# A stack of eight layers on one core: attention loops written out, side work of a selective scan moved

## The chip, the cores and the metric

The kernel runs on one core of a Trainium2 chip, as one launch. The metric is the device time of a run in microseconds (us), the median of three. The core has a matrix engine (TensorE, PE in the profile), a vector engine (VectorE, DVE), an activation engine (ScalarE, ACT), GpSimd (POOL) and SyncE (SP), which here issues the DMAs. Each engine works through its own list of instructions in order; they meet through semaphores. Matrix products go to PSUM, eight banks of 128 x 512 fp32.

## What is computed

2048 tokens of width 128 pass through eight layers, each with a layer norm ahead of it and a residual added: softmax attention, a mixture of experts, a selective scan, experts again, linear attention, other experts, gated linear attention, and those experts again. Cut to the two layers that the change touches:

```python
# softmax attention, 16 heads of width 8
keys, queries, values = x @ triu(Wk).T, x @ tril(Wq).T, x @ Wv.T
dot = einsum('bqhs,bkhs->bhqk', queries, keys) * scale
att = softmax(dot, axis=-1)
out = einsum('bhqk,bkhs->bqhs', att, values).reshape(b, t, e)
x = x + out @ Wu.T + bu

# selective scan, d_inner 256, d_state 16
xz = xn @ in_proj_w.T;  x_ssm, z = split(xz, 2)
x_ssm = silu(causal_conv4(x_ssm) + conv_b)
dt, B, C = split(x_ssm @ x_proj_w.T, [8, 24])
delta = softplus(dt @ dt_proj_w.T + dt_proj_b)
def step(h, (x_t, d_t, B_t, C_t)):
    h = exp(d_t * A) * h + (d_t * x_t) * B_t
    y_t = sum over states of h * C_t
y = y + x_ssm * Dp
out = (y * silu(z)) @ out_proj_w.T
```

## The kernel before

All activations stay on the core: 16 tiles of 128 tokens, in 4 chunks of 512. Every stage is one function with a block of code for each engine. The order of an engine's work is the order in which that block is written; there is no scheduler.

**softmax_attention.** It works in slots, one for each of the 16 key or query tiles of each of the 16 heads, 256 in all. The scores of a head are computed twice. In the first pass (`find`, L633) a tile of queries meets all keys, and VectorE takes the row maximum from PSUM in two halves (`maxima`, L828). At a head's end VectorE joins and transposes the maxima (L831, L835), GpSimd cuts them into three bf16 parts (`cut_max`, L534 to L547), and SyncE stores them and loads them into the stack of queries as extra rows (`store_max`, L456, L459). In the second pass (`score`, L648) a tile of keys meets all queries, the maximum already subtracted, into a ring of three banks; ScalarE takes the exponential (`unit`, L751) into a ring of four tiles, and TensorE multiplies it by the values (L665), whose second half of columns is ones, so that the sum for the softmax comes along. A slot of TensorE holds 4 `find`, 4 `score` and the value products, of three different tiles: the scores are `LAG_S` = 19 slots behind the maxima, the values 2 more. At the end of a head ScalarE copies the result out (`evacuate`, L758). Stacks and values have three buffers, so a loop body is three heads, 48 slots. The first body is written out with constants, bodies 1 to 4 are a hardware loop (`Fori`) on TensorE, ScalarE, GpSimd and SyncE, and the last head and the tail of the lag are written out again. VectorE loops head by head, from head 1.

ScalarE's unit, whose two waits come up later, is this (`unit`, L747 to L752):

```python
if not first:
    act.wait_ge(pv_done, j * BODY + (us - (RING - 1)))
for c in range(NC_):
    n = us * NC_ + c
    act.wait_ge(s_done, j * (4 * BODY) + (n + 1))
    nc.scalar.activation(probs[...], core.ps[:, S_BANK + n % S_RING, :], ACT.Exp)
```

**selective_scan.** Four chunks of 512 tokens, each 16 rounds (one for each state s), each round in two halves d of 128 channels. In a round ScalarE writes exp(delta * A) to PSUM (L1522), GpSimd multiplies delta * x by the row of B (L1279, B's rows come from DRAM through SyncE), VectorE runs the scan along the tokens (L1633) and multiplies the result by C (L1644), which TensorE has spread over the partitions (`spread_c`, L1355). TensorE adds the products of all states up in PSUM (`add_up`, L1362). ScalarE can be one round ahead of VectorE, GpSimd two.

Beside the rounds, at rounds set by numbers in the code, goes the side work. For z of this chunk and for x of the next one: a projection on TensorE (`find_z`, `convolve`), an open of four operations on ScalarE (`open_z`, `open_x`, L1449 to L1452), a sum on GpSimd (`sum_z` L1244, `sum_x` L1240), a close on ScalarE (L1469, L1461), a product on VectorE (`gate_z`, `gate_x`). Then B, C and the step size of the next chunk: `project_x`, `project_dt`, `copy_bc` (L1473, L1474), `open_dt`, `close_dt`, `take_delta` (L1593), `cut` and `join` (B and C in three bf16 parts), `weigh` (L1248). At a chunk's end TensorE adds the D term (x times D on a diagonal, L1429), VectorE multiplies by z (`finish`, L1601), TensorE projects out, VectorE adds to the residual (`add_out`).

The lead-in does for chunk 0 what the rounds do for the next chunk, and the layer norm of all four chunks: `stat_rows` (L1560 to L1566), `root` on GpSimd (L1221), `norm_rows` (L1572), `turn` and `copy_turned`.

## Time and profile before

| | us |
|---|---|
| three runs | 1780.85, 1781.93 (median), 1785.73 |
| the profiled run, as timed | 1789.17 |
| its span in the profile | 1787.4 |
| busy: TensorE, VectorE, ScalarE, GpSimd | 1542.1, 1401.7, 929.3, 394.0 |

The profile is one execution. Busy shares are averages over eight stages with different limits; what counts is which engine in a stage never waits, and for how long the others make it wait. Attention lasts from the start to about 730 us in the span, the selective scan from 911 to 1219 us. Timelines give for each group of like instructions the start, the length of the group, the engine, the line of the kernel, output and input, the count, and in brackets the idle time of that engine just before, with the engine and line that ended it.

### The profile page before, as it was taken

To read this page: it belongs to the slowest core of one execution; us is meant where nothing else is said; L and a number is where in the kernel's file an instruction comes from. 1 tells how busy PE (TensorE), PEld (TensorE's weight loads), DVE (VectorE), ACT (ScalarE), POOL (GpSimd) and SP (SyncE) were. 2 spreads that over 40 slices of the span, in tenths; PEclk is the share of its full clock that TensorE was granted. 3 is DMA by queue.
4 is the path that set the end of the run, shared out by engine and by line. 5 is a ranking of instruction groups with operands and counts; after the bars stand their busy time and mean duration, and the time that the engine had idled before them with its cause. 6 is when DMAs were issued, how large, how long until landed. Compare 5 with 4: busy or idle time off the path is not lost. (4 is left out here: it accounts for less than half of the span.)

```text
span 1787.4 us, 26936 instructions
## 1 busy us (share of the span) xinstructions
PE 1542.1 (86%) x8504; PEld 790.1 (44%) x8504; DVE 1401.7 (78%) x2392; ACT 929.3 (52%) x1758; POOL 394.0 (22%) x428
## 2 busy tenths in 40 slices
PE   7899999999999998599977887867998678786797
PEld 3112222222212211288842333325887567666576
DVE  6999998989989993476656999996765568489684
ACT  3188887878878888332235565543322322221221
POOL 3200000000000000000027777770000124232143
PEclk7599999999999999799988999998999879898799
DMA  3331000000000102000003221110000013100122
GB/s 112 128 110 29 24 22 23 23 24 22 23 23 24 34 12 48 8 1 1 1 1 77 61 66 65 62 51 0 1 1 1 1 49 95 49 1 1 49 86 82
DMA packets 41202, 66.58 MB, mean 37 GB/s; under 512 B 11374, under 2 KB 18335, under 8 KB 40344
## 3 DMA queue, kind: packets, MB, share of 16 engines
q1 hardware_dynamic: 41064, 64.82, 12.0%
q8 instruction: 77, 1.26, 0.3%
q14 instruction: 61, 0.50, 0.1%
HBM read 57.02 MB, written 6.88 MB: 36 GB/s over the span
## 5 line engine op out<-in xcount | busy, mean ns | idle before, releaser
L828 DVE TENSOR_REDUCE row_max<-ps 128x1 f32<-128x1024 f32 x512 | 601.7, 1219 | 52.2 <-PE ps L633 43.9
L751 ACT ACTIVATE probs<-ps 128x512 f32<-128x512 f32 x1024 | 530.2, 602 | 141.2 <-PE ps L648 140.5
L633 PE MATMUL ps<-k_stack,q_stack 48*128 48x512 bf16 x1024 | 327.2, 408 | 37.8 <-DVE row_max L828 12.7
L648 PE MATMUL ps<-q_stack,k_stack 51*128 51x512 bf16 x1024 | 343.3, 392 | 14.0 <-ACT probs L751 10.4
L665 PE MATMUL ps<-probs,v_head 128*16 128x512 f32 x2048 | 274.2, 608 | 0.0
L633 PEld LDWEIGHTS ps<-k_stack,q_stack 48*128 48x128 bf16 x1024 | 73.6, 96 | 386.2 <-DVE row_max L828 353.9
L1362 PE MATMUL ps<-s_hc,ident 128*128 128x512 f32 x256 | 145.0, 650 | 55.7 <-DVE s_hc L1644 55.7
L987 ACT ACTIVATE e_gate<-ps 128x512 f32<-128x512 f32 x128 | 76.3, 598 | 191.7 <-PE ps L220 191.7
L1279 POOL TENSOR_TENSOR s_dbx<-s_dx,s_b_rows 128x512 f32<-128x512 f32 x128 | 159.6, 1270 | 61.4 <-DVE s_h L1633 60.9
L1633 DVE TENSOR_TENSOR_SCAN s_h<-ps,s_state,s_dbx 128x512 f32<-128x512 f32 x128 | 156.8, 1265 | 11.4 <-ACT ps L1522 8.5
L1022 DVE TENSOR_TENSOR e_hidden<-e_gate,ps 128x512 f32<-128x512 f32 x128 | 87.7, 686 | 59.7 <-PE ps L220 47.1
L648 PEld LDWEIGHTS ps<-q_stack,k_stack 51*128 51x128 bf16 x1024 | 77.3, 94 | 112.6 <-ACT probs L751 107.2
L958 PEld LDWEIGHTS ps<-w_w,e_hidden 128*128 128x128 f32 x1024 | 123.2, 192 | 4.1
L958 PE MATMUL ps<-w_w,e_hidden 128*128 128x128 f32 x1024 | 125.0, 275 | 0.0
L1522 ACT ACTIVATE ps<-s_delta,s_a_neg 128x512 f32<-128x512 f32 x128 | 86.4, 687 | 66.0 <-DVE s_h L1633 65.7
L1994 ACT ACTIVATE m_gate<-ps 128x512 f32<-128x512 f32 (+1 forms) x72 | 43.0, 598 | 133.5 <-PE ps L220 133.5
L218 PE MATMUL ps<-e_x_high,e_w_high 128*128 128x512 f32 x256 | 106.9, 418 | 1.1 <-DVE e_hidden L1022 1.1
L1362 PEld LDWEIGHTS ps<-s_hc,ident 128*128 128x128 f32 x256 | 46.6, 200 | 128.4 <-DVE s_hc L1644 100.9
L1903 POOL TENSOR_TENSOR m_gate<-m_gate,m_spread 128x512 f32<-128x512 f32 x64 | 81.5, 1275 | 98.9 <-ACT m_gate L1994 56.8
L534 POOL TENSOR_TENSOR neg_max_parts<-neg_maxT,by_one 128x32 bf16<-128x32 f32 x16 | 4.0, 251 | 444.6 <-DVE neg_maxT L835 444.6
L1033 DVE SCALAR_TENSOR_TENSOR x_res<-ps,e_probs,x_res 128x128 f32<-128x128 f32 x256 | 72.1, 344 | 37.5 <-PE ps L958 37.2
L220 PE MATMUL ps<-e_x_low,e_w_high 128*128 128x512 f32 x256 | 101.4, 396 | 0.0
(354 smaller groups left out, 2103.8 us busy)
## 6 DMA issues: line engine op xcount, KB each, us to landing
s_b_rows<-s_b_dram SPq DMA_DIRECT2D x64, 256.0 KB, 3.1
m_spread<-m_probs_dram SPq DMA_DIRECT2D x128, 128.0 KB, 3.0
q_stack<-q_parts_dram SPq DMA_DIRECT2D x30, 96.0 KB
k_stack<-k_parts_dram SPq DMA_DIRECT2D x30, 96.0 KB
w_w<-w_dram SPq DMA_DIRECT2D x1, 2048.0 KB, 8.0
o_dram<-o_sb SPq DMA_DIRECT2D x64, 32.0 KB
q_stack<-q_parts_dram SPq DMA_DIRECT2D x30, 64.0 KB
k_stack<-k_parts_dram SPq DMA_DIRECT2D x30, 64.0 KB
```

Of the source, the lines that this page charges most:

```text
L218: nc.tensor.matmul(bank, self.w_high[:, u, cols], self.x_high[:, chunk], start=True, stop=False)
L220: return nc.tensor.matmul(bank, self.w_high[:, u, cols], self.x_low[:, chunk], start=False, stop=True)
L633: last = nc.tensor.matmul(core.ps[:, 2 * b + r, :], qst[buf][0:KROWS, u * P:(u + 1) * P], kst[buf][0:KROWS, key:key + CH], start=True, sto ...
L648: nc.tensor.matmul(core.ps[:, S_BANK + n % S_RING, :], kst[buf][HALF:ROWS, kt * P:(kt + 1) * P], qst[buf][HALF:ROWS, c * CH:(c + 1) * CH], ...
L665: last = nc.tensor.matmul(core.ps[32 * c:32 * c + VROWS, O_BANK, :], v_head[buf][:, kt, :], probs[:, m % RING, c * CH:(c + 1) * CH], start ...
L751: nc.scalar.activation(probs[:, us % RING, c * CH:(c + 1) * CH], core.ps[:, S_BANK + n % S_RING, :], ACT.Exp).then_inc(exp_done, 1)
L828: nc.vector.tensor_reduce(mx[:, u, b:b + 1], core.ps[:, 2 * b:2 * b + 2, :], mybir.AxisListType.XY, ALU.max).then_inc(max_done, 1)
L958: last = nc.tensor.matmul(core.ps[:, DOWN + n % 2, k * P:(k + 1) * P], hidden[n % 2][:, half, k * P:(k + 1) * P], w["w3"][:, e, half, :], ...
L1022: nc.vector.tensor_tensor(hidden[n % 2][:, half, :], gate[half][:], core.ps[:, UP + 2 * half + 1, :], ALU.mult).then_inc(hidden_done, 1)
L1279: nc.gpsimd.tensor_tensor(dbx[u % RING][:], dx[c % 2][d][:], b_rows[g % RING][:], ALU.mult).then_inc(dbx_done, 1)
L1362: nc.tensor.matmul(core.ps[:, Y_BANK + d, :], core.ident[:], hc[d][:], start=s == 0, stop=False).then_inc(summed, 1)
L1633: nc.vector.tensor_tensor_scan(out=h[g % 2][:, d, :], data0=core.ps[:, A_BANKS[d], :], data1=dbx[u % RING][:], initial=state[:, s, d:d + 1 ...
```

## The change

In attention the hardware loops of five engines become Python loops, so that all their instructions are written out, and `LAG_S` goes from 19 to 20 slots. In the scan the lead-in is reordered (VectorE makes the x gate of chunk 0 ahead of the statistics of chunks 2 and 3, cuts B and C of chunk 0 in GpSimd's place, TensorE runs 24 matmuls whose result nobody reads, `turn(2)` comes after the first step size), the D term goes from the end of a chunk to rounds 13 and 14, `finish` goes behind the first product of the next chunk, and the side work's rounds are shifted.

```diff
-    LAG_S = NT + 3
+    LAG_S = NT + 4
@@ SyncE, GpSimd, TensorE, ScalarE (four places)
-            with pe.Fori(1, LOOPED) as j:
+            for j in range(1, LOOPED):
@@ VectorE
-            maxima(0, 0)
-            with dve.Fori(1, HEADS) as i:
-                maxima(i, i * NT)
+            for head in range(HEADS):
+                maxima(head, head * NT)
@@ scan, GpSimd, lead-in
-            for c in range(1, NC_):
-                root(c)
+            root(1)
             for d in range(ND):
                 sum_x(0, d)
-            cut(0)
-            join(0)
+            for c in range(2, NC_):
+                root(c)
@@ scan, GpSimd, rounds
-                    if s in (4, 6):
-                        sum_z(c, s // 2 - 2)
+                    if s in (4, 5):
+                        sum_z(c, s - 4)
                     elif c + 1 < NC_:
-                        if s in (8, 10):
-                            sum_x(c + 1, s // 2 - 4)
+                        if s in (6, 8):
+                            sum_x(c + 1, s // 2 - 3)
@@ scan, TensorE
+            def add_skip(c, d):
+                nc.tensor.matmul(core.ps[:, Y_BANK + d, :], skip[:, d, :], xs[c % 2][d][:], start=False, stop=False)
...
             turn(1)
-            turn(2)
             pe.wait_ge(merged_copied, 1)
             pe.wait_ge(consts_set, 2)
+            for _ in range(24):
+                nc.tensor.matmul(core.ps[:, Z_BANKS[1], :], pick[:, 0, :], pick[:, 0:TPC, :],
+                                 start=True, stop=True)
             project_x(0, 0)
             project_dt(0, 0, 0)
             project_x(0, 1)
             project_dt(0, 0, 1)
+            turn(2)
...
+                        elif s == 7:
+                            project_x(c + 1, 0)
                         elif s == 8:
-                            project_x(c + 1, 0)
+                            project_dt(c + 1, 0, 0)
                         elif s == 9:
-                            project_dt(c + 1, 0, 0)
+                            project_x(c + 1, 1)
                         elif s == 10:
-                            project_x(c + 1, 1)
                             project_dt(c + 1, 0, 1)
...
+                    if s in (13, 14):
+                        if c == 0:
+                            pe.wait_ge(skip_set, ND)
+                        add_skip(c, s - 13)
                 for d in range(ND):
                     add_up(c, DS - 1, d)
-                    if c == 0 and d == 0:
-                        pe.wait_ge(skip_set, ND)
-                    nc.tensor.matmul(core.ps[:, Y_BANK + d, :], skip[:, d, :], xs[c % 2][d][:],
-                                     start=False, stop=True).then_inc(y_ready, 1)
@@ scan, ScalarE
-                    if s == 1:
+                    if s == 2:
                         open_z(c, 0)
                     elif s == 3:
                         close_z(c, 0)
                         open_z(c, 1)
-                    elif s == 5:
+                    elif s == 4:
                         close_z(c, 1)
...
                         if s == 5:
                             open_x(c + 1, 0)
+                        elif s == 6:
+                            close_x(c + 1, 0)
                         elif s == 7:
-                            close_x(c + 1, 0)
                             open_x(c + 1, 1)
-                        elif s == 9:
+                        elif s == 8:
                             close_x(c + 1, 1)
+                        elif s == 10:
+                            copy_bc(c + 1)
                         elif s == 11:
-                            copy_bc(c + 1)
                             open_dt(c + 1, 0)
@@ scan, VectorE
             def finish(c):
                 for d in range(ND):
-                    dve.wait_ge(y_ready, ND * c + d + 1)
+                    dve.wait_ge(summed, ND * DS * (c + 1) - ND + d + 1)
...
-            for c in range(NC_):
+            for c in range(2):
+                stat_rows(c)
+                norm_rows(c)
+            for d in range(ND):
+                gate_x(0, d)
+            for c in range(2, NC_):
                 stat_rows(c)
                 norm_rows(c)
             for c in range(NC_):
                 residual(c)
-            for d in range(ND):
-                gate_x(0, d)
+            cut_first()
...
-                    if s == 0 and c:
-                        finish(c - 1)
                     dve.wait_ge(c_spread, g + 1)
...
-                    if s == 2 and c:
+                    if s == 0 and c:
+                        finish(c - 1)
+                    elif s == 2 and c:
                         add_out(c - 1)
-                    elif s in (4, 6):
-                        gate_z(c, s // 2 - 2)
+                    elif s in (3, 4):
+                        gate_z(c, s - 3)
                     elif c + 1 < NC_:
-                        if s in (7, 9):
-                            gate_x(c + 1, (s - 7) // 2)
+                        if s in (6, 8):
+                            gate_x(c + 1, s // 2 - 3)
```

`cut_first` is new on VectorE and does for chunk 0 what `cut` and `join` did on GpSimd: two subtractions and two copies, of at most 96 x 512.

What the change moves on three engines, in the engines' own lists (line, operation, output and input, shape; the bracket names the semaphores that the instruction waits for).

ScalarE in attention, a unit of the loop body (a_pv counts value products, a_scores counts score matmuls). Before:

```order
L750 REGISTER_ALU [waits a_pv]
L751 ACTIVATE probs<-ps 128x512 [waits a_scores]
L750 REGISTER_ALU
L751 ACTIVATE probs<-ps 128x512 [waits a_scores]
L750 REGISTER_ALU
```

and now:

```order
L751 ACTIVATE probs<-ps 128x512 [waits a_scores,a_pv]
L751 ACTIVATE probs<-ps 128x512 [waits a_scores] x3
L751 ACTIVATE probs<-ps 128x512 [waits a_scores,a_pv]
L751 ACTIVATE probs<-ps 128x512 [waits a_scores] x3
L758 COPY o_sb<-ps 128x512 [waits a_o_stored,a_pv]
```

The register instructions are gone, and the wait for the values stands on the first exponential of each unit, beside the one for the scores.

TensorE in the scan's lead-in, from the first transposes on (L1301/L1298 turn, L1318/L1315 convolve, L1335 to L1345 or L1332 to L1342 projections). Before:

```order
L1301 MATMUL ps<-ident,xn 128x128 x4
L1318 MATMUL ps<-s_xnT,s_w_conv 128x512 x8
L1301 MATMUL ps<-ident,xn 128x128 x8
L1335 MATMUL ps<-s_xs,w_x_bc 96x512
L1343 MATMUL ps<-s_ones,w_dt_b 128x512
L1345 MATMUL ps<-s_xs,s_w_delta 128x512
L1335 MATMUL ps<-s_xs,w_x_bc 96x512
L1345 MATMUL ps<-s_xs,s_w_delta 128x512
L1343 MATMUL ps<-s_ones,w_dt_b 128x512
```

and now:

```order
L1298 MATMUL ps<-ident,xn 128x128 x4
L1315 MATMUL ps<-s_xnT,s_w_conv 128x512 x8
L1298 MATMUL ps<-ident,xn 128x128 x4
L1390 MATMUL ps<-w_pick 128x512 x24
L1332 MATMUL ps<-s_xs,w_x_bc 96x512
L1340 MATMUL ps<-s_ones,w_dt_b 128x512
L1342 MATMUL ps<-s_xs,s_w_delta 128x512
L1332 MATMUL ps<-s_xs,w_x_bc 96x512
L1342 MATMUL ps<-s_xs,s_w_delta 128x512
L1298 MATMUL ps<-ident,xn 128x128 x4
L1340 MATMUL ps<-s_ones,w_dt_b 128x512
```

The 24 matmuls stand between the second turn and the first projection, and the third turn has moved behind the first step size.

ScalarE in rounds 2 to 6 of a chunk (L1522/L1526 the exponentials, L1487/L1491 save, then open and close of z, first open of x). Before:

```order
L1522 ACTIVATE ps<-s_delta,s_a_neg 128x512 x2
L1487 COPY s_state<-s_h 128x2
L1469 ACTIVATE s_z_gate<-s_z_gate 128x512
L1449 ACTIVATE s_x_gate<-ps,w_conv_b 128x512
L1450 ACTIVATE s_x_gate<-s_x_gate 128x512
L1451 ACTIVATE s_x_gate<-s_x_gate 128x512
L1452 ACTIVATE s_below<-ps,s_neg_b 128x512
```

and now:

```order
L1473 ACTIVATE s_z_gate<-s_z_gate 128x512
L1526 ACTIVATE ps<-s_delta,s_a_neg 128x512 x2
L1491 COPY s_state<-s_h 128x2
L1453 ACTIVATE s_x_gate<-ps,w_conv_b 128x512
L1454 ACTIVATE s_x_gate<-s_x_gate 128x512
L1455 ACTIVATE s_x_gate<-s_x_gate 128x512
L1456 ACTIVATE s_below<-ps,s_neg_b 128x512
```

The close of z has moved out of round 5, where it stood between the save and the open of x, into round 4.

## Rows read from the trace of the kernel before

**Rows 1.** Timeline of ScalarE: start, length, operation, count, idle before

```profile
200.63 2.06 ACT L751 ACTIVATE probs<-ps 128x512 f32<-128x512 f32 x4 [0.38 <-PE ps L648]
...
203.01 2.07 ACT L751 ACTIVATE probs<-ps 128x512 f32<-128x512 f32 x4 [0.32 <-PE ps L648]
...
692.25 2.06 ACT L751 ACTIVATE probs<-ps 128x512 f32<-128x512 f32 x4 [0.37 <-PE ps L648]
```

**Rows 2.** Timeline of VectorE, the transposes at the ends of heads

```profile
113.13 0.21 DVE L835 STREAM_TRANSPOSE neg_maxT<-neg_max 128x32 f32<-128x32 f32 x1
...
152.92 0.21 DVE L835 STREAM_TRANSPOSE neg_maxT<-neg_max 128x32 f32<-128x32 f32 x1
...
643.75 0.21 DVE L835 STREAM_TRANSPOSE neg_maxT<-neg_max 128x32 f32<-128x32 f32 x1
...
682.87 0.21 DVE L835 STREAM_TRANSPOSE neg_maxT<-neg_max 128x32 f32<-128x32 f32 x1
```

**Rows 3.** Timeline of VectorE, first maxima after head 0 and head 14

```profile
73.02 14.18 DVE L828 TENSOR_REDUCE row_max<-ps 128x1 f32<-128x1024 f32 x12 [0.26 <-DVE neg_maxT L835]
...
644.39 14.09 DVE L828 TENSOR_REDUCE row_max<-ps 128x1 f32<-128x1024 f32 x12 [0.43 <-PE ps L633]
```

**Rows 4.** Waits of TensorE (total, times, longest us); timeline of ScalarE

```profile
PE ps L633 <- issue: 7.8, 3, 2.7
...
273.95 2.06 ACT L751 ACTIVATE probs<-ps 128x512 f32<-128x512 f32 x4 [3.16 <-PE ps L648]
...
323.62 2.06 ACT L751 ACTIVATE probs<-ps 128x512 f32<-128x512 f32 x4 [1.90 <-PE ps L648]
```

**Rows 5.** Timeline of VectorE: a scan round without side work

```profile
993.00 2.45 DVE L1633 TENSOR_TENSOR_SCAN s_h<-ps,s_state,s_dbx 128x512 f32<-128x512 f32 x2
...
996.54 2.45 DVE L1633 TENSOR_TENSOR_SCAN s_h<-ps,s_state,s_dbx 128x512 f32<-128x512 f32 x2
```

**Rows 6.** Waits of VectorE, 920 to 1195 us (total, times, longest)

```profile
DVE s_h L1633 <- ACT ps L1522: 8.5, 10, 1.5
...
DVE s_yT L1601 <- PE ps L1429: 5.2, 5, 1.6
```

**Rows 7.** Timelines around round 3 of chunk 1: GpSimd, ScalarE, VectorE

```profile
1030.50 1.27 POOL L1244 TENSOR_TENSOR s_z_gate<-s_z_gate,s_below 128x512 f32<-128x512 f32 x1
...
1031.81 0.63 ACT L1469 ACTIVATE s_z_gate<-s_z_gate 128x512 f32<-128x512 f32 x1 [1.82 <-POOL s_z_gate L1244]
...
1030.85 2.45 DVE L1633 TENSOR_TENSOR_SCAN s_h<-ps,s_state,s_dbx 128x512 f32<-128x512 f32 x2
...
1035.35 2.46 DVE L1633 TENSOR_TENSOR_SCAN s_h<-ps,s_state,s_dbx 128x512 f32<-128x512 f32 x2 [0.88 <-ACT ps L1522]
...
1044.19 2.46 DVE L1633 TENSOR_TENSOR_SCAN s_h<-ps,s_state,s_dbx 128x512 f32<-128x512 f32 x2 [1.06 <-ACT ps L1522]
```

**Rows 8.** Timeline of VectorE at the end of chunk 0

```profile
1015.73 2.45 DVE L1633 TENSOR_TENSOR_SCAN s_h<-ps,s_state,s_dbx 128x512 f32<-128x512 f32 x2
...
1023.16 2.45 DVE L1633 TENSOR_TENSOR_SCAN s_h<-ps,s_state,s_dbx 128x512 f32<-128x512 f32 x2
```

**Rows 9.** Timeline of VectorE at the end of the last chunk

```profile
1214.15 0.69 DVE L1601 TENSOR_TENSOR s_yT<-ps,s_zs 128x512 f32<-128x512 f32 x1 [1.48 <-PE ps L1429]
```

**Rows 10.** Timeline of the lead-in: VectorE and ScalarE

```profile
921.71 0.86 DVE L1560 BATCH_NORM_STATS2 s_stats<-x_res 128x6 f32<-128x128 f32 x4
...
926.04 0.87 DVE L1560 BATCH_NORM_STATS2 s_stats<-x_res 128x6 f32<-128x128 f32 x4
...
927.86 0.67 ACT L1452 ACTIVATE s_below<-ps,s_neg_b 128x512 f32<-128x512 f32 x1
...
950.88 2.47 DVE L1633 TENSOR_TENSOR_SCAN s_h<-ps,s_state,s_dbx 128x512 f32<-128x512 f32 x2 [2.83 <-POOL s_dbx L1279]
```

**Rows 11.** Windows of the lead-in: busy us by engine, TensorE's granted clock, DMA

```profile
929.00:931.00 2.00, 0.00 (x0) 0.00 (x0) 1.66 (x2) 0.44 (x1) 2.00 (x3) 1.00 0.00 0
...
939.00:941.00 2.00, 2.00 (x3) 0.62 (x2) 0.00 (x0) 0.00 (x0) 0.00 (x0) 0.50 0.00 0
```

21 lines of the change are left out of this document (15 added, 6 removed).

## The prediction

> **What bounds the kernel now.** The page gives the span, 1787.4 us; the profiled run took 1789.17 us, the median of the runs shown is 1781.93 us. I sum against the profile and take the difference off the median. Two of the eight stages change: softmax attention, to about 730 us, and the selective scan, from 911 to 1219 us. I read first the timelines of VectorE and ScalarE there, then the waits.
>
> *Attention.* The unit is a slot: 4 max-pass matmuls, 4 score matmuls, 4 value matmuls on TensorE, 2 row maxima on VectorE, 4 exponentials on ScalarE. ScalarE shows the cycle: four exponentials in about 2.07 us, then a short wait for the next score. The sum of both is the slot. Look at that wait: 0.38 us up to the unit at 200.63, 0.32 from 203.01 on, and 0.37 again at 692.25 [rows 1]. Those are the units 0 to 48, 49 to 239 and 240 on: exactly the units before, in and after ScalarE's loop (units 48 to 239; the first unit in the loop still shows the old gap). TensorE enters its loop 19 slots before ScalarE enters its own and leaves it as much before, and nothing moves there. So the slot is 2.45 us where ScalarE's code is written out and 2.39 us in its loop. VectorE's own need is a little less, 14.18 us for 12 maxima, 2.36 us a slot [rows 3]. Reader, keep this: the loop is the faster form inside a body, and loses at its ends.
>
> Heads are read from VectorE's transposes, one at each head's end: 113.13 to 152.92 is a head in written-out pace, 39.79 us; 152.92 to 682.87 are 13 heads, 529.95 us [rows 2]. The ends of the loops are in these: TensorE's returns ("issue", 7.8 us in 3 times) leave ScalarE idle 3.16 us at 273.95, and ScalarE's own return leaves 1.90 us at 323.62 [rows 4].
>
> *Scan.* A round without side work takes 996.54 - 993.00 = 3.54 us [rows 5], all of it VectorE: two scans, two products. VectorE also waits 8.5 us in 10 times for ScalarE's exponentials and 5.2 us for the sum in PSUM at chunk ends [rows 6].
>
> **The change part by part.**
>
> *Loops written out.* Added: no arithmetic. Removed: branches, register work. All 13 heads then run at the written-out pace, if nothing else changes: 13 x 39.79 = 517.3 against 529.95, so -12.7 us. This is a net. The last head in the loop, 643.75 to 682.87, takes 39.12 us; at that pace without loop ends 13 heads would save 21.4 us, and the slower exponentials take 8.7 of it back (13 x 0.67). The order rows show what the slower form is: written out, the first exponential of a unit waits for two semaphores itself; in the loop the wait for the values sits on a register instruction ahead of it. Bounds for this term: -21.4 (pace of the loop kept, ends gone) and -6 (VectorE's waits slow down as ScalarE's do and eat the 0.09 us a slot that it has in hand). I take -12.7, from the nearest rows, heads run in this very form.
>
> *VectorE's loop per head.* Between a transpose and the next maximum it idles 0.43 us in the loop, 0.26 after head 0, which is written out [rows 3]. Both lie on the path, for VectorE is then late and the next scores behind it. Worth 0.2 us x 13 = -2.6 us; between 0 and -5.6 (0.43 x 13).
>
> *One slot more lag.* Scores, exponentials and values of a head come a slot later. The stack of the row maxima gets a slot more to arrive; who waited for that once gains what is already in the 13 heads. The price: one more slot of the tail without maxima, 2.07 + 0.37 = 2.44 us [rows 1], less 0.09 us for one more slot at VectorE's own pace at the start: +2.35. SyncE's stack loads of a head are released a slot later and had many slots in hand, so they cost nothing.
>
> *Scan, side work.* ScalarE's round holds two exponentials and a save; the four operations that open a gate (2.5 us) just fit beside them, a close waiting for GpSimd and an open do not. In round 3 the close starts at 1031.81, after GpSimd's sum from 1030.50; the open behind it delays the scan at 1035.35 by 0.88 us [rows 7]. In rounds 5 and 7 the same: 1.06 (the row at 1044.19) and 0.4 us. The change puts x's close in the round after its open, so rounds 5 to 8 have one of them each: I take these six waits as gone, about 4.4 of the 8.5 us [rows 6]; each late round also starts 0.08 us later than a plain one: -4.9. Round 3 keeps close and open, but VectorE now does z's first gate product there, 0.6 us of work in the gap: 4 x 0.6 = -2.4. Sum -7.3; bounds -10 and -3.
>
> *Chunk ends.* The D term no longer stands behind the last sum, and the products with z come after the first product of the new chunk. From the scan at 1015.73 to the one at 1023.16 are 7.43 us [rows 8]; work is 3.54 + 2 x 0.6 = 4.74. Saved 2.7, once more at the third end, 0.3 at the second: -5.7; bounds -6 and -3. The D matmuls stand in rounds 13 and 14, where TensorE waits for VectorE anyway. At the very end the product waits 1.48 us [rows 9] and the next one too, for two sums and two D terms of 0.86 us; without the latter -1.7.
>
> *Lead-in.* Before: the first scan at 950.88 [rows 10]. After, worked forward on VectorE, which becomes the chain: the second open ends at 927.86 + 0.67 = 928.5; GpSimd's sum, now not behind two root computations, 1.25 -> 929.8; close 0.63 -> 930.5; gate 0.7 (as the product in [rows 9]) -> 931.2; chunks 2 and 3 at 4.33 us each (926.04 - 921.71) -> 939.9; residual factors 0.6 -> 940.5; the cut of B and C, four operations now on VectorE, 2.4 -> 942.9; two deltas 1.3 -> 944.2; GpSimd's products 1.26 each, the first beside the second delta, -> 946.2; B product 1.26 -> 947.5. So -3.3. The cut is in no row of VectorE; four ops of 0.2 to 0.7 us with their waits are 1.5 to 3.0. TensorE: 24 fillers from 926.5 on, where it idles now, still granted the full clock at 929 and half of it, 1.2 GHz, at 939 [rows 11]. At full clock they take 24 x 0.21 = 5.1 us, projections and step sizes are ready near 939.5, under VectorE's chain. At half clock they take 10.2 us and the step size is the end again: then only -0.9. Copies and GpSimd's work are each earlier than their readers.
>
> The VectorE page of the Trainium skill ("VectorE: DVE Perf Modes", section "The perf-mode tier table") says that a copy from SBUF runs in a faster mode than a two-input operation. By it the cut's two copies would be its cheap half and its end near 942.5, an estimate by that page that shifts the lead-in by some 0.4 us; no row here shows a copy of this shape on VectorE.
>
> **Sum.** -12.7 - 2.6 + 2.35 = -12.9 in attention; -7.3 - 5.7 - 1.7 - 3.3 = -18.0 in the scan. Together -31: span 1756, median 1751 us.
>
> **Rivals.**
> 1. *The loop's pace is kept*: the 0.06 us belongs to something other than the two waits (a phase between engines). For: only a coincidence of two switches speaks for the form. Against: both switches fall on ScalarE's loop borders and on no other engine's. 1751 - 8.7 = 1742.
> 2. *The scan keeps half its waits*: a side operation a round later meets another one, for instance the z sum on GpSimd ahead of the B product. For: the orders of four engines were shifted against each other. Against: GpSimd has about a microsecond free in a round. Half of 14.7 us comes back: 1758.
> 3. *Fillers at half clock*: TensorE ends the lead-in; +2.4: 1753. It is granted the full clock up to 931 even when idle [rows 11], and the fillers follow at once.
> 4. *Slower: written-out code must be fetched.* TensorE's return to a loop start costs up to 2.7 us [rows 4]. If straight code paid that too, the 192 slots that are now written out would need 14 such stops, one in 14 slots, to lose the 31 us and 5 more; there the time is 1751 + 14 x 2.7 = 1789, at one in 8 slots 1816. Against: the first 48 slots are straight code now, and the head from 113.13 to 152.92 shows only its regular waits.
> The Trainium skill ("Runtime: NRT & Kernel Launch", section "Instruction fetch mechanics") says that blocks are prefetched in straight code, mostly hidden, and that a taken branch breaks this; by it rival 4 costs nothing, by the opposite reading it is this rival. The trace agrees with the page at the loop returns.
> 5. *No effect of writing out* (the stops at loop ends come from elsewhere): then the slower form is all that writing out adds, 13 x 0.67 = +8.7, with the lag's +2.35 and the scan's -18 a total of -7: 1775. Against: the waits of 3.16 and 1.90 us stand in the very slots where the loops of TensorE and ScalarE return.
>
> **Chances.** Forecast 0.58 (1746 to 1757 with its own bounds); rival 1 0.14; rival 2 0.13; rival 3 0.07; rival 5 0.04; rival 4 0.04. Rival 1 and the low bounds reach to 1738, rival 2 with the high bounds to 1763; about 2 in 10 lie outside. A change under 0.3%, 5 us, is about what cannot be told from none: faster 0.93 (rival 5 is -7 us), same 0.04, slower 0.03.
>
> **What would show it.** ScalarE's wait of 0.37 to 0.38 us in all slots and heads 39.5 to 39.8 us apart; no waits above 1 us in attention; 22 slots after the last transpose; plain rounds at 3.54 us with waits for ScalarE of 0.3 us in round 4 alone; no wait at chunk ends; TensorE at full clock until about 940 and the first scan near 947.6. Wrong would be: heads at 39.2 (rival 1), a stall at equal steps of instructions in attention (rival 4), new waits for GpSimd in rounds 4 to 8 (rival 2).

## The result

The changed kernel takes 1754.12 us (median of 4 runs, 1752.69 to 1755.01), the kernel before 1783.83 us (4 runs, 1780.85 to 1786.18). The ratio is 0.9834, with a 95% interval of 0.9814 to 0.9853: faster by 29.7 us. I had predicted 1751 us, between 1738 and 1763, and a gain of 31 us.

The profiled runs lie further apart: 1787.4 us of span before, 1751.0 after, 36.4 us. The profiled run of before took 1789.17 us, more than any of its four timed runs; the one of after took 1752.69 us, its fastest. So the sum of the prediction, made against the profile, is compared with the profile here, and the 7 us between the two measures have their own part below.

In attention, ScalarE's gap is 0.38 us now in the unit at 287.11, where before it was 0.32 [rows 1]; heads are 39.34 us apart. The timeline of the changed kernel, ScalarE and then VectorE (start, length, operation, count, idle before):

```profile
287.11 2.06 ACT L751 ACTIVATE probs<-ps 128x512 f32<-128x512 f32 x4 [0.38 <-PE ps L648]
...
692.55 2.06 ACT L751 ACTIVATE probs<-ps 128x512 f32<-128x512 f32 x4 [0.37 <-PE ps L648]
...
151.79 0.21 DVE L835 STREAM_TRANSPOSE neg_maxT<-neg_max 128x32 f32<-128x32 f32 x1
...
270.33 16.70 DVE L828 TENSOR_REDUCE row_max<-ps 128x1 f32<-128x1024 f32 x14
...
663.50 0.21 DVE L835 STREAM_TRANSPOSE neg_maxT<-neg_max 128x32 f32<-128x32 f32 x1
```

The waits of its TensorE between 95 and 690 us (total, times, longest):

```profile
PE ps L633 <- DVE row_max L828: 5.8, 14, 0.4
PE ps L648 <- ACT probs L751: 3.8, 12, 0.5
```

What the reader is to see: "issue", 7.8 us before [rows 4], is gone from TensorE's waits, and the maxima at 270.33 begin right behind the transpose at 270.09, with no idle time in front; before there were 0.43 us [rows 3].

In the scan, VectorE's waits for ScalarE between 936 and 1180 us, which answer to [rows 6]:

```profile
DVE s_h L1654 <- ACT ps L1526: 1.7, 4, 0.9
```

VectorE's timeline in the lead-in, at the end of chunk 0 and at the end of the last chunk ([rows 10], [rows 8], [rows 9]):

```profile
895.80 0.87 DVE L1566 BATCH_NORM_STATS2 s_stats<-x_res 128x6 f32<-128x128 f32 x4 [1.87 <-PEq L81]
...
913.58 0.75 DVE L1589 SCALAR_TENSOR_TENSOR s_xs<-ps,w_conv_b,s_x_gate 128x512 f32<-128x512 f32 x1 [7.27 <-ACT s_x_gate L1465]
...
924.99 0.68 DVE L1617 TENSOR_TENSOR s_rest<-s_full,s_bc 96x512 f32<-96x512 f32 x1
925.70 0.42 DVE L1619 CAST s_mid<-s_rest 96x512 bf16<-96x512 f32 x1
926.16 0.28 DVE L1621 COPY s_bc<-s_mid 32x512 bf16<-32x512 bf16 x1
926.48 0.68 DVE L1623 TENSOR_TENSOR s_bc<-s_rest,s_mid 32x512 bf16<-32x512 f32 x1
927.19 1.29 DVE L1599 SCALAR_TENSOR_TENSOR s_delta<-ps,s_soft 128x512 f32<-128x512 f32 x2
931.93 2.47 DVE L1654 TENSOR_TENSOR_SCAN s_h<-ps,s_state,s_dbx 128x512 f32<-128x512 f32 x2 [3.46 <-POOL s_dbx L1276]
...
994.54 2.45 DVE L1654 TENSOR_TENSOR_SCAN s_h<-ps,s_state,s_dbx 128x512 f32<-128x512 f32 x2
...
998.09 1.28 DVE L1607 TENSOR_TENSOR s_yT<-ps,s_zs 128x512 f32<-128x512 f32 x2
999.28 2.44 DVE L1654 TENSOR_TENSOR_SCAN s_h<-ps,s_state,s_dbx 128x512 f32<-128x512 f32 x2
...
1181.07 0.69 DVE L1607 TENSOR_TENSOR s_yT<-ps,s_zs 128x512 f32<-128x512 f32 x1 [0.62 <-PE ps L1359]
```

The scans around a chunk end are 999.28 - 994.54 = 4.74 us apart, 7.43 before [rows 8]; the product with z runs in between without a wait.

Where the 36.4 us are, by landmarks of the two traces:

| stretch | before | after | gain | forecast |
|---|---|---|---|---|
| start to the third transpose (152.92) | 152.92 | 151.79 | 1.1 | none |
| 13 heads, to the last transpose | 529.95 | 511.71 | 18.2 | 12.7 + 2.6 |
| last transpose to the last output copy | 47.46 | 49.91 | -2.45 | -2.35 |
| to the first statistics of the scan | 180.96 | 182.39 | -1.4 | none |
| lead-in, to the first scan | 39.59 | 36.13 | 3.5 | 3.3 |
| first to last scan | 258.17 | 244.89 | 13.3 | 7.3 + 5.7 |
| last scan to the update of x_res | 9.65 | 7.94 | 1.7 | 1.7 |
| all the rest | 568.7 | 566.2 | 2.5 | none |

The -1.4 and the 2.5 us lie in stages that no edit touches. Over the traces of all kernels here they last 180.6 to 182.6 and 563.5 to 569.2 us, so both are spread between executions.

### The profile page after: what moved, and what is told of

It reads as the page before. It is cut to its first block and busy times, and to the rows that moved or that the text cites. A ratio compares the mean times of both kernels' runs of the same rounds, so it can differ in the third digit from the quotient of the medians.

```text
span 1751.0 us, 24117 instructions
## 1 busy us (share of the span) xinstructions
PE 1542.9 (88%) x8528; PEld 772.8 (44%) x8528; DVE 1398.6 (80%) x2396; ACT 928.4 (53%) x1758; POOL 390.9 (22%) x424
## 5 line engine op out<-in xcount | busy, mean ns | idle before, releaser
L633 PE MATMUL ps<-k_stack,q_stack 48*128 48x512 bf16 x1024 | 325.0, 402 | 20.3 <-DVE row_max L828 10.6
L665 PE MATMUL ps<-probs,v_head 128*16 128x512 f32 x2048 | 269.6, 599 | 0.0
L633 PEld LDWEIGHTS ps<-k_stack,q_stack 48*128 48x128 bf16 x1024 | 58.5, 95 | 367.8 <-DVE row_max L828 341.8
L1359 PE MATMUL ps<-s_hc,ident 128*128 128x512 f32 x256 | 138.5, 626 | 49.4 <-DVE s_hc L1663 44.4
L1526 ACT ACTIVATE ps<-s_delta,s_a_neg 128x512 f32<-128x512 f32 x128 | 87.3, 689 | 79.6 <-DVE s_h L1654 77.6
L219 PE MATMUL ps<-e_x_high,e_w_low 128*128 128x512 f32 x256 | 101.5, 397 | 0.0
```

The source lines that it names most:

```text
L219: nc.tensor.matmul(bank, self.w_low[:, u, cols], self.x_high[:, chunk], start=False, stop=False)
L633: last = nc.tensor.matmul(core.ps[:, 2 * b + r, :], qst[buf][0:KROWS, u * P:(u + 1) * P], kst[buf][0:KROWS, key:key + CH], start=True, sto ...
L665: last = nc.tensor.matmul(core.ps[32 * c:32 * c + VROWS, O_BANK, :], v_head[buf][:, kt, :], probs[:, m % RING, c * CH:(c + 1) * CH], start ...
L1359: nc.tensor.matmul(core.ps[:, Y_BANK + d, :], core.ident[:], hc[d][:], start=s == 0, stop=s == DS - 1).then_inc(summed, 1)
```

## Experiments: the two halves

The experiments ran in three sessions, each with the kernel before beside them (medians 1783.00, 1784.66 and 1781.32 us). The changed kernel was not run again in them, so a distance to it of 2 or 3 us shows nothing by itself; the traces have to carry such a reading.

**Attention alone.** The kernel before with the five loops of attention written out and the lag of 20:

```diff
-            with act.Fori(1, LOOPED) as j:
+            for j in range(1, LOOPED):
...
-    LAG_S = NT + 3
+    LAG_S = NT + 4
```

> The kernel before with the attention part of the change alone (loops of all five engines written out, score lag 20 slots, value lag 22), scan as before. Theory (the written-out pace holds in all slots and the loops' ends go): the last output copy of attention comes about 16.9 us earlier than in the profile of before, at 713.4, as in the profile of the changed kernel; the scan keeps its 39.6 us lead-in and 258.2 us from first to last scan; time about 1783.8 - 16 = 1768. Rival (the stages lean on each other, for instance by what is in flight when the scan's code begins): attention saves less than 13 us or the scan changes, and the two halves do not add up to the whole.

Measured: 1770.03 us, 13.0 under the 1783.0 of before on that chip (ratio 0.9929, 0.9913 to 0.9946). Attention's last output copy comes at 714.02, 16.3 us earlier, heads at 39.34. The theory's 1768 is missed by 2 us, and its scan of 258.2 us by 3.9 (254.29), of which more below.

**Scan alone.** The other half, with `LAG_S` and all `Fori` of attention as before.

> The changed kernel with the attention part undone (loops and lag as before): the scan part alone. Theory: first to last scan 244.9 us against 258.2, lead-in to the first scan 36.1 against 39.6, end 7.9 against 9.6 us: together -18.4, time about 1765. With the other half (-16) that is 34 us, more than the 29.7 by which the timed runs differ: so either the timed runs of before lack some 5 us of attention that its profiled run shows, or one half is smaller on the clock than in the profile. Rival (halves overlap): this half gives 13 to 14 us only, about 1770.

Measured: 1769.11 us, 13.9 under before (0.9922, 0.9906 to 0.9939). Lead-in 36.59 us, first to last scan 245.06, end 7.94: 17.8 us in the trace. The theory's stretches came and its time, 1765, did not: 13.9 us and 1769 is what the rival had said. The halves add up to 26.9 us, against 29.7 for the whole, within what the intervals allow, so these runs show no overlap; what is missing against the traces is explained next.

**Why the timed gain is smaller than the traced one.** The scan of the first run is the scan of before, word for word, yet it takes 254.29 us from first to last scan, not 258.17. The difference is at the chunk ends. First a window at the end of chunk 0 in the kernel before (busy us of each engine, then TensorE's granted clock, DMA share, GB/s):

```profile
1016.00:1018.00 2.00, 2.00 (x4) 0.69 (x3) 2.00 (x2) 0.75 (x2) 1.57 (x2) 0.50 0.28 94
```

Its timeline there, a pair of TensorE's matmuls (L1429 is the D product) and VectorE's second product with z:

```profile
1017.13 1.92 PE L1429 MATMUL ps<-s_xs,s_skip 128*128 128x512 f32 x2
...
1021.36 0.69 DVE L1601 TENSOR_TENSOR s_yT<-ps,s_zs 128x512 f32<-128x512 f32 x1 [1.58 <-PE ps L1429]
```

The same window, one chunk end, in the run with attention alone changed:

```profile
1000.00:1002.00 2.00, 2.00 (x6) 0.80 (x6) 2.00 (x3) 0.95 (x2) 1.59 (x3) 1.00 0.28 99
```

And its timeline (the D product is L1428 here):

```profile
1000.25 1.02 PE L1428 MATMUL ps<-s_xs,s_skip 128*128 128x512 f32 x2
...
1003.02 0.69 DVE L1600 TENSOR_TENSOR s_yT<-ps,s_zs 128x512 f32<-128x512 f32 x1 [0.74 <-PE ps L1428]
```

In the trace of before, chunks 0 and 2 end while TensorE is at 1.2 GHz (0.50), and the second product with z waits 1.58 and 1.52 us; chunk 1 ends at 2.4 GHz and it waits 0.24. With attention alone changed, it waits 0.74, nothing and 0.24 us. So what an end costs before depends on a clock that differs from run to run. With the change the work of a chunk end is off VectorE's path: the traces of the changed kernel, of the scan alone and of the run without value wait all show no wait at the three ends. The ends make 3.9 us of difference between two executions of the same scan.

There are 4.2 us more in attention. The run with the scan alone has the attention of before, word for word, and its last output copy comes at 726.09 us, in the profile of before at 730.33. Of these 4.2 us, 1.6 are in one head, 478.20 to 518.96, which takes 40.76 us in the profile of before and 39.18 in the other. In it a score waits for the stack of the row maxima to come from memory, the longest such wait in any trace here:

```profile
486.82 0.38 PE L648 MATMUL ps<-q_stack,k_stack 51*128 51x512 bf16 x1 [1.20 <-DMA q_stack<-max_dram]
```

Most of the others are around the returns of the loops. I read from both that the profile of before was a dear execution by some 8 us against the two runs that share its halves, which covers the 7 us between the traced and the timed gain; its timed runs have no trace, so that they were cheaper in these places is inferred, not shown. Over all sessions before ran from 1778.95 to 1789.09.

## Experiments: the pace of attention

**No value wait.** ScalarE no longer waits for the values of an older unit; the first score implies it, as TensorE issues both in order.

```diff
             def unit(j, us, first=False):
-                if not first:
-                    act.wait_ge(pv_done, j * BODY + (us - (RING - 1)))
                 for c in range(NC_):
```

> The changed kernel without ScalarE's wait for the values ahead of each unit's exponentials: the wait for the first score of the unit implies it, since TensorE issues the values of three units before ahead of that score. Arithmetic and order are unchanged; only the second wait of each first exponential goes. Theory (two waits on one exponential are the 0.06 us): ScalarE's gap falls from 0.38 to 0.32 us, slot 2.387 us, heads 38.4 to 38.7 us apart (VectorE's own floor is near 38.3), tail of 22 slots 1.3 us shorter; time about 1754 - 16 x 0.8 - 1 = 1741. Rival 1 (written-out code is fetched as it runs and the fetch costs the 0.06): gap 0.38, heads 39.34, time 1754. Rival 2 (a phase between engines): gap anywhere between, and different in different heads.

Measured: 1742.39 us, ratio 0.9768 (0.9752 to 0.9784), 12 us below the changed kernel. The timeline, ScalarE and VectorE:

```profile
286.40 2.07 ACT L749 ACTIVATE probs<-ps 128x512 f32<-128x512 f32 x4 [0.32 <-PE ps L648]
...
344.53 0.21 DVE L833 STREAM_TRANSPOSE neg_maxT<-neg_max 128x32 f32<-128x32 f32 x1
...
383.14 0.21 DVE L833 STREAM_TRANSPOSE neg_maxT<-neg_max 128x32 f32<-128x32 f32 x1
```

The gap is 0.32 us in straight code: neither the loop nor fetching makes the difference, the second wait does. Heads are 38.62 us apart.

**The wait on the fourth exponential.** As many double waits, on another instruction.

```diff
-                if not first:
-                    act.wait_ge(pv_done, j * BODY + (us - (RING - 1)))
                 for c in range(NC_):
                     n = us * NC_ + c
+                    if c == NC_ - 1 and not (first and us < RING - 1):
+                        act.wait_ge(pv_done, j * BODY + (us + 1 - (RING - 1)))
...
-                    unit(j, us, first and us < RING)
+                    unit(j, us, first)
```

> The changed kernel with the value wait of a unit moved from its first exponential to the fourth exponential of the unit before. There are as many double waits as in the changed kernel, but on an exponential that follows another with nothing to wait for. Theory (a second wait costs only where the instruction stands at the head of the queue with an idle engine behind it, as it does on the first exponential): gap 0.32 us, four exponentials in 2.06 us, heads 38.62, time as without the wait, 1742. Rival (a second wait costs 0.06 us wherever it stands): four exponentials in 2.12 us or the gap at 0.38, heads 39.34, time 1754.

Measured: 1742.02 us (0.9781, 0.9755 to 0.9806), heads 38.61. ScalarE's timeline:

```profile
288.18 2.06 ACT L751 ACTIVATE probs<-ps 128x512 f32<-128x512 f32 x4 [0.32 <-PE ps L648]
```

A second wait costs 0.06 us on the instruction that an idle engine waits for, and nothing on one that has work in front of it and whose conditions are long met. That it is so the two runs show; what in the engine makes it so stays open.

**ScalarE's loop alone.** `with act.Fori(1, LOOPED) as j:` back, all else as changed.

> The changed kernel with ScalarE's attention code alone back in its loop (3 passes of 48 units and a written-out part at both ends); the other four engines stay written out. Theory (the loop's form moves the second wait to a register instruction): gap 0.32 us in units 48 to 239, and three returns that leave ScalarE idle 1.7 to 1.9 us each, 1.4 us net a return: 192 x 0.057 = -10.9, + 4 = about -6, time 1748; heads between returns 38.4 to 38.7 us. Rival (the pace is set by something else and the loop only adds its returns): heads 39.34 and time 1754 + 4 = 1758.

Measured: 1752.53 us, 4 above the theory's 1748 and level with the changed kernel. The gap is 0.32 us in the loop and 0.38 outside, heads 38.70, as forecast. Two terms were off: the heads between returns gain 0.64 us each (38.70 against 39.34), where 192 x 0.057 makes 0.91 a head, and the returns were priced too low. ScalarE's timeline at the first head that has one:

```profile
315.01 2.06 ACT L751 ACTIVATE probs<-ps 128x512 f32<-128x512 f32 x4 [0.32 <-PE ps L648]
318.75 2.06 ACT L751 ACTIVATE probs<-ps 128x512 f32<-128x512 f32 x4 [1.68 <-PE ps L648]
322.02 2.06 ACT L751 ACTIVATE probs<-ps 128x512 f32<-128x512 f32 x4 [1.20 <-PE ps L648]
```

The first return makes two late units, at 318.75 and at 322.02; the three heads with one are 41.23, 41.48 and 40.03 us, 6.6 us more than 38.70 each, where I had taken 4. The third return stops ScalarE as long as the first, but no unit behind it is late:

```profile
556.22 2.06 ACT L751 ACTIVATE probs<-ps 128x512 f32<-128x512 f32 x4 [1.65 <-PE ps L648]
```

What differs is TensorE's granted clock, in a window behind each of the two:

```profile
320.00:322.00 2.00, 2.00 (x12) 0.29 (x6) 0.00 (x0) 0.82 (x2) 0.00 (x0) 0.50 0.00 0
...
558.00:560.00 2.00, 1.95 (x16) 0.53 (x16) 1.19 (x2) 1.68 (x4) 0.00 (x0) 1.00 0.00 0
```

Behind the first it is 1.2 GHz (0.50) until about 323, behind the third it stays at 2.4 GHz. The returns cost 2.53 and 1.33 us, so by these two rows the half clock is about 1.2 us of the first.

**TensorE's loop alone.** `with pe.Fori(1, LOOPED) as j:` back, all else as changed.

> The changed kernel with TensorE's attention code alone back in its loop. In the run with ScalarE's loop alone three returns cost 2.5, 2.8 and 1.3 us. In the profile of before both engines' returns cost about 18 us together (heads of 43.0, 40.8, 43.1, 40.6, 43.9, 41.7 and 40.8 us against 39.2). Theory (TensorE's return is the dear one, and each engine pays its own): three intervals of 39.34 + 3 to 4 us, in all +10 to +12, time 1765; slots stay at 0.38 us gaps. Rival (the stalls come when several engines return within a few slots of one another): below +5 here, time under 1759.

Measured: 1775.4 us (ratio 0.9958, 0.9943 to 0.9974), 21 above the changed kernel. The sign is the theory's, the size twice it: heads with a return are 46.27, 46.79 and 45.53 us against 39.42. The timeline of TensorE and ScalarE behind the first return:

```profile
273.36 0.38 PE L633 MATMUL ps<-k_stack,q_stack 48*128 48x512 bf16 x1 [3.54 <-issue]
...
273.95 2.06 ACT L751 ACTIVATE probs<-ps 128x512 f32<-128x512 f32 x4 [4.10 <-PE ps L648]
...
276.57 1.91 PE L665 MATMUL ps<-probs,v_head 128*16 128x512 f32 x8 [1.36 <-ACT probs L751]
...
279.12 2.06 ACT L751 ACTIVATE probs<-ps 128x512 f32<-128x512 f32 x4 [3.10 <-PE ps L648]
```

And a window there, with the granted clock behind the busy times:

```profile
276.00:278.00 2.00, 1.43 (x8) 0.15 (x8) 0.42 (x1) 0.02 (x1) 0.00 (x0) 0.50 0.03 6
```

TensorE issues nothing for 3.54 us, ScalarE stands 4.10 us, and then the clock is granted at half until about 281, so that 8 value matmuls take 1.91 us in place of 1.05 and the next score is late by another 3.10. The stall of 3.54 us is half of this return's price of 6.85. Not all of the rest is the clock: within the 3.10 us lies a second stop, 1.36 us in which TensorE stands ahead of the value matmuls. The profile puts it down to the exponentials, but the code has these matmuls wait for a unit whose exponentials had ended before 268 us, so it was something else. At the other two returns the stops are 3.53 and 1.14, and 3.66 and 0.87 us, which leaves, by subtraction, 1.6 to 2.7 us a return for the slots at half clock. The Trainium skill ("Runtime: NRT & Kernel Launch", section "Instruction fetch mechanics") says that a taken branch out of the prefetched blocks stalls the engine; the rows agree with it, and the straight code of the changed kernel shows no such stall.

The kernel before has the same half clock behind the return and no second stop. Its timeline, TensorE and ScalarE:

```profile
275.14 1.91 PE L665 MATMUL ps<-probs,v_head 128*16 128x512 f32 x8
...
277.63 2.06 ACT L751 ACTIVATE probs<-ps 128x512 f32<-128x512 f32 x4 [1.61 <-PE ps L648]
```

There TensorE's three stalls are 2.41, 2.64 and 2.73 us, and heads with its return are 3.8, 3.9 and 4.7 us longer than 39.2. So the theory's 3 to 4 us was a fair reading of the kernel before, and a return costs TensorE more when the other engines are written out. Why its stall is then a microsecond longer, and what the second stop waits for, no run here shows. The loops of GpSimd and SyncE were not put back alone.

**VectorE's loop per head alone.**

```diff
-            for head in range(HEADS):
-                maxima(head, head * NT)
+            maxima(0, 0)
+            with dve.Fori(1, HEADS) as i:
+                maxima(i, i * NT)
```

> The changed kernel with VectorE's maxima alone back in their loop per head. The heads of the changed kernel are 39.34 us apart where written-out heads of before are 39.79. Theory (VectorE's turn at a head's end is on the path): its idle time after each transpose comes back, 0.2 to 0.45 us a head, heads 39.55 to 39.8, time 1754 + 3 to 7 = 1757 to 1761. Rival (the 0.45 us a head came with the longer lag, because the stack of maxima landed late for the first score of a head): heads stay at 39.34, time 1754.

Measured: 1759.99 us, heads 39.72, within the theory's ranges, and the gap behind each transpose is back, in VectorE's timeline:

```profile
312.20 0.21 DVE L835 STREAM_TRANSPOSE neg_maxT<-neg_max 128x32 f32<-128x32 f32 x1
312.83 16.70 DVE L828 TENSOR_REDUCE row_max<-ps 128x1 f32<-128x1024 f32 x14 [0.43 <-PE ps L633]
```

**The lag back at 19.** `LAG_S = NT + 3`, loops written out.

> The changed kernel with the score lag back at 19 slots (value lag 21), all loops written out. Theory of the prediction (the lag costs one slot of tail, 2.35 us, and gives nothing else): heads 39.34, 21 slots after the last transpose, time 1754 - 2.4 = 1751.7. Rival (the stack of maxima lands some 6.3 us after the transpose, in the changed kernel at 355.05 for the transpose at 348.77, and with 19 slots the first score of each head waits for it, 0.3 to 0.6 us, and VectorE behind it): heads 39.7 to 39.9, which is +0.45 x 15 - 2.4 = +4.4, time 1758.

Measured: 1754.42 us (1749.72 to 1755.79), the same as the changed kernel. From the last transpose to the last copy are 47.48 us, 2.43 less, as the theory says. The heads stay at 39.34 and none of them waits for the stack, so the rival falls for all but the first; there it holds, in TensorE's timeline:

```profile
79.70 0.60 PE L648 MATMUL ps<-q_stack,k_stack 51*128 51x512 bf16 x1 [0.20 <-DMA q_stack<-max_dram]
```

No kernel with 20 slots waits there. The transpose of head 1 comes at 113.28 against 112.44, and it came between 112.27 and 113.07 in the other kernels with 20 slots and everything written out. So the shorter lag gives back some tenths of a microsecond at the start; that this is all that keeps the time from falling is not shown, for the traced run was the fastest of the four, and 2 us are below what these runs resolve.

## Experiments: the scan

**D term back at the end.**

```diff
-                    if s in (13, 14):
...
-                        add_skip(c, s - 13)
                 for d in range(ND):
                     add_up(c, DS - 1, d)
...
+                    nc.tensor.matmul(core.ps[:, Y_BANK + d, :], skip[:, d, :], xs[c % 2][d][:],
+                                     start=False, stop=True).then_inc(y_ready, 1)
...
-                    dve.wait_ge(summed, ND * DS * (c + 1) - ND + d + 1)
+                    dve.wait_ge(y_ready, ND * c + d + 1)
```

> The changed kernel with the D term back behind the last sum of each chunk, and VectorE's product with z waiting for it, at its new place after the first product of the next chunk. Theory (the new place of the product hides sums and D term when TensorE runs at full clock; only the last chunk has nothing to hide behind): no wait at chunk ends at full clock, up to 1 us at an end that finds TensorE at 1.2 GHz; the last chunk's end 1.7 us later; time 1754 + 1.7 to 3 = 1756 to 1757. Rival (the D term itself is what was waited for): each of three ends is 1 to 2 us longer, + 1.7: time 1759 to 1762.

Measured: 1759.87 us (ratio 0.9870, 0.9847 to 0.9892); first to last scan 251.92 us against 244.89, the end 9.67 against 7.94. My theory was wrong and the rival's price right, by a way that neither had named. A window at the end of chunk 2:

```profile
1124.00:1126.00 2.00, 2.00 (x3) 0.94 (x4) 2.00 (x3) 1.02 (x2) 1.57 (x2) 0.50 0.37 104
```

The timeline of TensorE and VectorE there:

```profile
1125.63 1.92 PE L1434 MATMUL ps<-s_xs,s_skip 128*128 128x512 f32 x2
...
1128.71 1.02 PE L1434 MATMUL ps<-s_xs,s_skip 128*128 128x512 f32 x2
...
1129.57 0.38 PE L1353 MATMUL ps<-s_bc,w_pick 96*128 96x512 bf16 x1
...
1129.99 1.29 DVE L1664 TENSOR_TENSOR s_hc<-s_h,ps 128x512 f32<-128x512 f32 x2 [3.31 <-PE ps L1353]
```

The D products stand ahead of the C row of the next chunk (L1353) in TensorE's queue. VectorE's product with C waits for that row, 3.31 us here at 1.2 GHz, 0.52 and 1.26 at the other two ends, together 5.1 of the 7.0 us. So at the three inner ends it is not the product with z that needs the D term gone, but what is queued behind it; at the last end the product with z waits for it, 1.48 us.

**Side work back in its rounds.** All opens, sums, closes, gates and projections as before; the lead-in and the chunk ends as changed.

```diff
-                    if s == 2:
+                    if s == 1:
                         open_z(c, 0)
...
-                        if s in (6, 8):
-                            gate_x(c + 1, s // 2 - 3)
+                        if s in (7, 9):
+                            gate_x(c + 1, (s - 7) // 2)
```

> The changed kernel with the side work of the rounds (gates' opens, sums, closes, products with the gates, projections, copies of B and C) back in the rounds and on the places of before on all engines; lead-in, D term, chunk ends and attention as changed. Theory (the term of the prediction, 7.3 us): VectorE waits for ScalarE's exponentials 8 to 8.5 us in 10 times again, first to last scan 244.9 + 7.3 = 252.2, time 1761.4. Rival (the waits came with the chunk ends' phase, and the new places do little): under 248 us and under 1757.

Measured: 1762.09 us (ratio 0.9887, 0.9866 to 0.9910), 8.0 above the changed kernel, first to last scan 252.14 us, 7.25 more, as the theory says, and the ten waits are back among VectorE's (total, times, longest):

```profile
DVE s_h L1651 <- ACT ps L1525: 8.5, 10, 1.5
```

**No fillers.** The 24 matmuls on `pick` left out; they compute nothing that is used.

> The changed kernel without the 24 matmuls that keep TensorE busy in the lead-in of the scan. In the changed kernel TensorE is granted the full clock up to 928, and the step sizes are ready at 926.06, 1.1 us before VectorE takes them at 927.19. Theory (the fillers hold the clock, and VectorE's chain has 1.1 us in hand): the projections after the gate run at 1.2 GHz, the step sizes come 2.5 to 4 us later, first scan 1.4 to 3 us later, time 1755.5 to 1757. Rival (the clock would not fall, or VectorE's chain covers it): first scan 36.1 us after the first statistics as now, time 1754.

Measured: 1755.97 us (1754.72 to 1756.58; the changed kernel was at most 1755.01). The lead-in is 38.70 us long, which looks like the theory. It is not. VectorE's timeline at the first gate product and the first scan:

```profile
915.33 0.75 DVE L1586 SCALAR_TENSOR_TENSOR s_xs<-ps,w_conv_b,s_x_gate 128x512 f32<-128x512 f32 x1 [9.85 <-ACT s_x_gate L1462]
...
933.68 2.47 DVE L1651 TENSOR_TENSOR_SCAN s_h<-ps,s_state,s_dbx 128x512 f32<-128x512 f32 x2 [3.13 <-POOL s_dbx L1276]
```

A window between them:

```profile
920.00:922.00 2.00, 2.00 (x3) 0.65 (x3) 1.21 (x5) 0.00 (x0) 0.76 (x1) 0.50 0.00 0
```

From the gate product to the scan are 18.35 us, and in the changed kernel too (913.58 to 931.93), though TensorE runs at half clock from 918 to 924 here: VectorE's chain is just long enough to cover the late step size. The 2.6 us are lost ahead of the place where the fillers stand, in the convolutions behind the first transposes: TensorE is at half clock for some 7 us at the start of the scan in ten of the fourteen traces and for some 10 us in this one, and also in the run with the D term at the end (20.41 us to the gate product, with its fillers) and the one with the side work undone (19.76), against 17.8 to 18.2 in the others with this lead-in. The fourth is the run with attention alone changed, whose scan is that of before, where the profile of before has 7. That is a clock that differs between executions, not the edit. The 1.9 us between the timed runs are too few to say more.

**The best of it together.** No value wait, lag 19, and both first products of step size and x on VectorE:

```diff
-            for d in range(ND):
-                weigh(0, d)
...
             for d in range(ND):
                 take_delta(0, d)
+                dve.wait_ge(delta_done, d + 1)
+                nc.vector.tensor_tensor(dx[0][d][:], delta[0][d][:], xs[0][d][:], ALU.mult).then_inc(dx_done, 1)
```

> The changed kernel with three edits that the runs and the trace point to: no value wait ahead of the exponentials (1742.4 alone), the score lag back at 19 slots, and in the lead-in of the scan both first products of step size and x on VectorE, each behind its step size (0.6 us each in a place where it idles 3.46 us) in place of GpSimd (2.49 us for two). Theory: heads 38.62, 21 slots after the last transpose (-2.4 us), first scan 34.0 to 34.4 us after the first statistics instead of 36.1; time 1742.4 - 2.4 - 1.9 = 1738. Rival (with the faster slots 19 of them are too few for the stack of maxima, which lands 6.3 us after the transpose while three slots now last 7.15): heads 38.8 to 39.2, which gives back 3 to 9 us, time 1741 to 1747.

Measured: 1743.92 us (0.9782, 0.9762 to 0.9803), 6 above the theory's 1738 and no better than the value wait's removal alone. Heads 38.62 and 46.35 us behind the last transpose are as expected, so the rival falls for the heads. Head 1's transpose comes later again (113.70), behind a first score that waits 0.55 us for the stack, and the first scan comes 17.85 us behind the gate product instead of 18.35, a gain of 0.5 us and not of 1.9. GpSimd's timeline:

```profile
917.99 7.39 POOL L1272 TENSOR_TENSOR s_dbx<-s_dx,s_b_rows 128x512 f32<-128x512 f32 x6 [6.67 <-DVE s_dx L1637]
```

GpSimd waits for both products before its first one with B, and VectorE now makes them one behind the other. The stages behind the scan, which no edit touches, took 569.2 us in this trace and 566.3 in the one without the value wait, so a gain of 1 or 2 us would not show in the time either. The best kernel is the changed one without its value wait, or with that wait on the fourth exponential: 1742 us.

## Why the prediction was right, and where it was not

*Right by its own steps.* Straight code keeps ScalarE's gap of 0.37 to 0.38 us in all slots, TensorE's returns go, and the net of both was the 12.7 us. Against the profile of before it is 13.3 (529.95 - 516.63, the 13 heads of the run with VectorE's loop alone). But the price was read from one execution: in the run with the scan alone, the same code, the 13 heads take 526.17 us, and against those the net is 9.5. So 3.8 us of what I put down to the loops did not come back in a second trace, 1.6 of them a wait for the stack of maxima. The removal of the wait and its move to the fourth exponential show the cause of the 0.06 us that I had only read from the order of instructions. Rival 1 is thereby out for this kernel, but its number, 1742, is what the kernel takes once the double wait is gone. Rival 4 (fetching) and rival 5 (the stops come from elsewhere) are out: no wait above 1 us in attention, and TensorE's loop alone brings back 21 us. Rival 3 is out too, since the 24 fillers take 5.34 us, which is full clock, and rival 2, since no wait for GpSimd appears in rounds 4 to 8.

*VectorE's loop per head*, put at 2.6 us: mis-sized. I took the 0.26 us of the written-out boundary behind head 0 as what would stay, and nothing stays; the run with that loop alone costs 0.38 us a head, 39.72 against 39.34. That is 4.9 us for 13 heads, and with 12.7 for the rest it makes 17.6 of the 18.2 measured.

*The loops' own prices* in the sum were a net; taken apart, ScalarE's three returns cost 6.6 us and TensorE's 20.3, each alone. In the kernel before both together cost less than that sum, and less than TensorE's alone (its eight heads from 271.55 to 604.56 are 19.4 us longer than 39.2 each).

*Side work and chunk ends* fit: 13.0 forecast, 13.3 measured, and the side work alone 7.25 where I had 7.3. The wait left in round 4 is 0.29 us in chunks 1 to 3 as forecast, and 0.88 in chunk 0, which I had not set apart. What I missed is that [rows 8] was taken at half clock, so that 5.7 us is the gain against that profile and less against a usual run.

*Lead-in*: 3.3 forecast, 3.5 measured, and VectorE's chain step by step within 0.3 us. I had put the cut's four operations at 2.4 us. They take 2.2 (924.99 to 927.19), with the two copies as the cheap ones, 0.42 and 0.28 against 0.68, as the Trainium skill ("VectorE: DVE Perf Modes", section "The perf-mode tier table") says. But the step on the fillers was wrong in its point: I had them hold the clock for the projections, and without them nothing is later by the first scan. And TensorE was at full clock to about 929 after (its window 928 to 930 is granted 0.80), which is 944 on the clock of before.

*Profile and median.* I subtracted from the profile and took the difference off the median, as if what the profile showed were in every execution. It was not, by some 4 us in attention and 4 in the scan. Attention was put at 12.9 us; the traces give 16.9 (1.1 + 18.2 - 2.45) and the timed run of that half 13.0, so what VectorE's loop was priced too low and what the profile had too much cancel. The scan was put at 18.0; the traces give 18.5 and the timed run of that half 13.9, so there the forecast is too high. The sum of 31 fell short of the traced 36.4 and hit the timed 29.7: part of the agreement is luck.

## What to carry to other kernels

Look at which instruction an engine stands idle on, and let that instruction wait for one semaphore only: a wait that another one implies, or one that is long met, belongs on an instruction behind it. Price a loop return by what follows it too, the stall and then the slots at half clock, and take the price from more than one execution. When an operation is moved off the end of a chunk, ask what stood behind it in the queue, not only who read its result.

## What the runs showed of the hardware

- An exponential with two waits starts 0.06 us later than one with one, if the engine is idle ahead of it (0.38 against 0.32 us); on an exponential with work ahead the second wait costs nothing.
- A TensorE return over a body of 48 slots costs 6.1 to 7.4 us where the other engines are written out, of which 3.5 to 3.7 us are the stall and 0.9 to 1.4 a second stop; heads with one are 3.8 to 4.7 us longer in the kernel before, where the others loop too. ScalarE's alone costs 1.3 to 2.8 us: 1.33 with the clock at 2.4 GHz behind it, 2.53 with 1.2.
- TensorE's granted clock is not the same at one place of the scan in all executions of the same code: chunk ends at 1.2 or 2.4 GHz, and 7 or 10 us of half clock at the start of the lead-in. That moves the scan of before by 3.9 us from first to last scan and the changed lead-in by up to 2.6.
